# A fused attention and FP4-feed-forward layer: each block of P times V issued as two halves by queries, behind the third and the fourth softmax tile of a key block

## The chip, the cores and the metric

The kernel runs on one core of a Trainium2 chip. The metric is the device time of one execution in microseconds (us), as the median of the runs shown. A profiled execution gives the rows that are read below.

## The reference, cut to what matters

```python
# x (4, 2048, 256), 16 heads of 16, rotary tables for the last 1369 positions
qkv = (x @ w_qkv + b_qkv).reshape(b, n, 3, H, DH).transpose(2, 0, 3, 1, 4)
...
attn = softmax(einsum('bhqd,bhkd->bhqk', q, k) * scale)      # 64 heads, each 2048 x 2048
out = einsum('bhqk,bhkd->bhqd', attn, v)
x = layernorm(x + out @ w_proj + b_proj)
# feed-forward: inputs and weights rounded blockwise to FP4
x = layernorm(x + fp4_linear(silu(fp4_linear(x, w_gate)) * fp4_linear(x, w_up), w_down))
```

## The kernel before, in words

The kernel has three stages: the projections with the rotary step (up to about 330 us), attention over 64 heads (to about 3100 us), and the output projection with the feed-forward part. The change lies in the attention stage alone. There the code is written out straight, head after head, and each engine works through its own queue in the order in which it is written. Engines wait for each other by semaphores.

TensorE (PE in the profile) does three kinds of work in this stage:

- **S tiles** (`s_tile`, line 563): 128 queries against 512 keys, from partitions 64 and up of `qst` and `kst`. They serve only to find each query's maximum. Two S tiles fill two neighbouring banks of PSUM. VectorE (DVE) then reduces the pair to one maximum for each query (line 927, 128x1024 elements). There are four S banks, so two pairs. The first tile of a pair waits for `s_done`, that is for the reduction of the pair two before. Here the pair of the first two S tiles of a key block is called **the first pair**, the other **the second pair**.
- **T tiles** (`t_tile`, line 594): 128 keys against 512 queries, with the maxima as extra rows, from partitions 0 to 50 of the same tiles. ScalarE (ACT) takes the exponential of each into `pt` (line 772) and counts `p_ready`. The T tiles go through three banks in turn, so each T tile waits until ACT has read the third one before it (`t_bank_free`).
- **P times V** (`pv`, line 605): the 128x32 block of V (16 columns of V, one of ones for the sums, the rest zero) against 2048 queries, in four matmuls of 512 queries. Each goes to its own 32 partitions of bank 7, so the four use different columns of the array. They are float32, and each leaves two MATMUL records, so a call of `pv` shows as x8. The last matmul counts `pv_step`.

A **key block** is 128 keys, 16 in a head (`KT`). In `head`, each key block issues S, T four times over, the S tiles for a later head (20 tiles ahead), and then the `pv` of the key block before. S and T tiles use different rows of the array, and run side by side. Here S1 to S4 and T1 to T4 are the tiles of a key block in that order. S3 is the one that waits for the reduction of the second pair of the key block before.

Two places in each head differ from that pattern. In key block 1 (the second), `pv` starts a new head and so waits for `o_out`, the copy of the last head's result out of bank 7. ACT makes this copy (line 763) behind the first exponential of that key block. In key block 12, behind T4, TensorE transposes the maxima of the next head (`m_tile`, line 584, which also takes a T bank). In the last head no S tiles are left, and in the one before only 11 of 16 key blocks have them.

Of the kernel before, what the change touches and what calls it, by code (L numbers as in the profile page):

```python
# [31 lines left out]
G = B * H  # L32
# [6 lines left out]
CHUNK = 512  # L39
CHUNKS = N // CHUNK  # L40
NCH = B * CHUNKS
KT = N // P
# [20 lines left out]
TILES_S = KT * CHUNKS  # L63
PAIRS = TILES_S // 2
S_BANKS, T_BANKS, O_BANK = 4, 3, 7
# [2 lines left out]
AHEAD = 20  # L68

M_AFTER = 51  # L70
VAR_STEPS = 6
LN_STEPS = 6

# [35 lines left out]
def wait_after(eng, sem, value):  # L109

    if not isinstance(value, int) or value > 0:
        eng.wait_ge(sem, value)
# [37 lines left out]
def t_place(g, i):  # L150

    return 1 + g * (TILES_S + 1) + i + (i > M_AFTER)


def m_place(g):

    return 0 if g == 0 else 1 + (g - 1) * (TILES_S + 1) + M_AFTER + 1

# [16 lines left out]
def each_head(fn):  # L175

    for g in range(G):
        fn(At(0, g))


def layer_kernel(nc, x, xT, sinT, cosT, w_qk, w_v, b_qk, b_v, w_proj, b_proj, w_gate, w_up, w_down, eye, out):
    nc.disable_value_cache = True
    ctx = ExitStack()
    with ctx:
# [3 lines left out]
        def sem(name):  # L188
            return ctx.enter_context(nc.semaphore(name))
# [11 lines left out]
        ps = ctx.enter_context(nc.psum_tensor("ps", [P, 8, 512], F32))  # L201
# [66 lines left out]
        pt = [take(N) for _ in range(2)]  # L268
        vs = [take(KT * 32, "p (t d) -> p t d", t=KT) for _ in range(2)]
# [48 lines left out]
        mt_psum, mt_out, t_psum, p_ready = (sem(n) for n in ("mt_psum", "mt_out", "t_psum", "p_ready"))  # L318
        pv_step, v_staged, o_out, inverted = (sem(n) for n in ("pv_step", "v_staged", "o_out", "inverted"))
# [171 lines left out]
        def _(pe):  # L491
# [62 lines left out]
            def s_tile(g, i):  # L554

                pair = i // 2
                if i == 0:
                    pe.wait_ge(s_in[g.u % 2], g.quad(128, 64 * (g.u // 2 + 1)))
                if i % 2 == 0 and not (g.static(0) and pair < 2):
                    pe.wait_ge(s_done, g.times(PAIRS, pair - 1))  # L560
                qt, kc = i // CHUNKS, i % CHUNKS
                q, k = qst[g.u % 2], kst[g.u % 2]
                mm = nc.tensor.matmul(ps[:, i % S_BANKS, :], q[SROW:SROW + STACK, qt * P:(qt + 1) * P],  # L563
                                      k[SROW:SROW + STACK, kc * CHUNK:(kc + 1) * CHUNK], start=True, stop=True)
                if i % 2:
                    mm.then_inc(s_psum, 1)

            def t_bank_free(place):
# [5 lines left out]
                g, i = divmod(back - 1, TILES_S + 1)  # L574
                if back == 0 or i == M_AFTER + 1:
                    pe.wait_ge(mt_out, 1 if back == 0 else g + 2)
                else:
                    pe.wait_ge(p_ready, g * TILES_S + i - (i > M_AFTER) + 1)

            def m_tile(g):  # L580

                pe.wait_ge(m_split, g + 1)
                t_bank_free(m_place(g))
                nc.tensor.transpose(ps[0:MROWS * KT, t_bank(m_place(g)), 0:P // 2].bitcast(BF16),
                                    mp[g % 2].rearrange("p j q -> p (j q)"), ident16[:, :]).then_inc(mt_psum, 1)

            def t_tile(g, kb, qb):

                i = kb * CHUNKS + qb
                if i == 0:  # L590
                    pe.wait_ge(t_in[g.u % 2], g.quad(128, 64 * (g.u // 2 + 1)))
                    pe.wait_ge(m_in[g.c % 2], 16 * MROWS * (g.c // 2 + 1))
                t_bank_free(t_place(g.c, i))
                nc.tensor.matmul(ps[:, t_bank(t_place(g.c, i)), :], kst[g.u % 2][0:ROWS, kb * P:(kb + 1) * P],  # L594
                                 qst[g.u % 2][0:ROWS, qb * CHUNK:(qb + 1) * CHUNK],
                                 start=True, stop=True).then_inc(t_psum, 1)

            def pv(g, kb):

                if kb == 0:  # L600
                    pe.wait_ge(v_staged, g.times(1, 1))
                    wait_after(pe, o_out, g.times(1))
                pe.wait_ge(p_ready, g.times(TILES_S, CHUNKS * (kb + 1)))
                for qb in range(CHUNKS):
                    mm = nc.tensor.matmul(ps[32 * qb:32 * qb + 32, O_BANK, :], vs[g.u % 2][:, kb, :],  # L605
                                          pt[kb % 2][:, qb * CHUNK:(qb + 1) * CHUNK],
                                          start=(kb == 0), stop=(kb == KT - 1))
                mm.then_inc(pv_step, 1)

            def head(g):  # L610


                nxt, after = g.back(-1), g.back(-2)
                for kb in range(KT):
                    for qb in range(CHUNKS):
                        i = kb * CHUNKS + qb + AHEAD
                        if i < TILES_S and not g.static(G - 1):
                            s_tile(nxt, i)
                        elif i >= TILES_S and not g.static(G - 1) and not g.static(G - 2):
                            s_tile(after, i - TILES_S)  # L620
                        t_tile(g, kb, qb)
                        if kb * CHUNKS + qb == M_AFTER and not g.static(G - 1):
                            m_tile(g.c + 1)
                    if kb:
                        pv(g, kb - 1)
                    elif not g.static(0):
                        pv(g.back(1), KT - 1)

            for i in range(TILES_S):
                s_tile(At(0, 0), i)  # L630
# [5 lines left out]
            pe.wait_ge(v_out, 2 * NCH)  # L636
            pe.wait_ge(bias_done, 1)
            each_head(head)
            pv(At(0, G - 1), KT - 1)


            pe.wait_ge(o_out, G)
# [54 lines left out]
        def _(act):  # L697
# [54 lines left out]
            def maxima(g):  # L752

                act.wait_ge(mt_psum, g + 1)
                if g >= 2:
                    act.wait_ge(m_in[g % 2], 16 * MROWS * (g // 2))
                nc.scalar.activation(m_rows[g % 2], ps[0:MROWS * KT, t_bank(m_place(g)), 0:P // 2].bitcast(BF16), ACT.Copy
                                     ).then_inc(mt_out, 1)

            def out_of_psum(g):  # L760
                act.wait_ge(pv_step, g.times(KT, KT))
                act.wait_ge(o_store[g.u % 2], g.quad(32 * CHUNKS, 16 * CHUNKS * (g.u // 2 + 1)))
                nc.scalar.activation(ost[g.u % 2], ps[:, O_BANK, :], ACT.Copy).then_inc(o_out, 1)

            def head(g):
                for kb in range(KT):

                    wait_after(act, pv_step, g.times(KT, kb - 1))
                    for qb in range(CHUNKS):
# [4 lines left out]
                        if not g.static(0) and kb == 1 and qb == 0:  # L774
                            out_of_psum(g.back(1))
                        if i == M_AFTER and not g.static(G - 1):
                            maxima(g.c + 1)
# [45 lines left out]
            def deviation(n, alone):  # L823
                if group := norm_group(n, alone):
                    e, cols = group
                    act.wait_ge(var_step, e.quad(VAR_STEPS, VAR_STEPS))
                    nc.scalar.activation(std[:, cols], var[:, cols], ACT.Sqrt).then_inc(std_done, 1)
# [9 lines left out]
        def _(dve):  # L837
# [110 lines left out]
            def variance(n, alone):  # L948
# [5 lines left out]
                e, cols = group  # L954
                at = lambda k: e.quad(VAR_STEPS, k)
                g_bn, g_var, g_sums, g_d = bn[:, cols], var[:, cols], sums[:, cols], ln_d[:, cols]
# [230 lines left out]
```

## Time and profile before

| | us |
|---|---|
| median of 3 runs | 3880.2 (3878.26 to 3880.56) |
| the profiled execution, its own time | 3876.52 |
| its span in the trace | 3874.7 |
| busy: TensorE matmuls / VectorE / ScalarE | 3617.4 / 3350.5 / 2527.9 |
| attention stage, by T1 of the first head and the last T4 | 330.8 to 3097.9 |
| span of one head by its first S load (1500.58 to 1543.79) | 43.21 |

PEld is TensorE's load of weights, which can overlap with PE, its matmuls. A row of the timeline has the start, the duration, the engine, the line, what is written and read, and in brackets the engine's idle time ahead and what ended it. The ends of matmuls are modelled. A merged row (x8) spans from the first start to the last end.

### The profile page before, as it was taken

The numbers are of one execution on the slowest core, as the hardware profiler recorded it, in microseconds if no ns is written. First come the engines' busy times: TensorE is split into PE (matmuls) and PEld (weight loads), VectorE is DVE, ScalarE is ACT, GpSimd is POOL, SyncE is SP. The second block draws the span as 40 slices with busy tenths as digits, with TensorE's granted clock in tenths as the row PEclk, the third lists the DMA queues.
The fourth block names the chain that finished last, engine by engine and source line by source line (L and its number), as shares of the span: only waits on it lengthen the run. The fifth ranks groups of instructions, "written<-read, shape, count | busy, mean of one in ns | idle before, by whom it ended". The sixth has DMA issues, their size and how long they took to land.

```text
span 3874.7 us, 56176 instructions
## 1 busy us (share of the span) xinstructions
PE 3617.4 (93%) x19560; PEld 1556.6 (40%) x19560; DVE 3350.5 (86%) x3879; ACT 2527.9 (65%) x4870; POOL 712.0 (18%) x883
## 2 busy tenths in 40 slices
PE   7769999999999999999999999999999978888887
PEld 4433333333333333333333333333333346656665
DVE  7998888888888888888888888888888379999997
ACT  4334777777777777777777777777777723333333
POOL 6870000000000000000000000000000045555554
PEclk9887999999999999999999999999999989999999
DMA  5441111111111111111111111111111111111110
GB/s 153 161 167 53 44 39 38 44 45 40 37 43 45 41 37 42 46 42 37 40 47 42 38 39 48 42 38 38 46 44 39 29 50 45 43 47 45 47 37 20
DMA packets 121153, 195.55 MB, mean 50 GB/s; under 512 B 28640, under 2 KB 83040, under 8 KB 108640
## 3 DMA queue, kind: packets, MB, share of 16 engines
q1 hardware_dynamic: 111712, 184.16, 14.2%
q10 hardware_dynamic: 9216, 8.39, 0.6%
q8 instruction: 140, 2.29, 0.2%
q14 instruction: 85, 0.70, 0.1%
HBM read 139.55 MB, written 51.38 MB: 49 GB/s over the span
## 4 chain that ended last, share of the span: by engine, by line
PE 70%; issue 10%; POOL 8%; DVE 7%; ACT 3%; DMA 1%; POOLq 0%; SPq 0%; ACTq 0%; DVEq 0%
PE ps L563 28%; PE ps L605 26%; PE ps L594 14%; POOL v_all L1130 2%; ACT arena L772 2%; DVE arena L904 2%; DVE arena L909 1%; POOL arena L1130 1%; POOL arena L1132 1%; POOL arena L1124 1%; POOL arena L1125 1%; DVE arena L927 1%; PE ps L679 1%; DVE arena L897 1%; POOL arena L1065 1%
## 5 line engine op out<-in xcount | busy, mean ns | idle before, releaser
L927 DVE TENSOR_REDUCE arena<-ps 128x1 f32<-128x1024 f32 x2048 | 2412.7, 1220 | 332.8 <-PE ps L563 326.5
L772 ACT ACTIVATE arena<-ps 128x512 f32<-128x512 f32 x4096 | 2122.0, 604 | 622.5 <-PE ps L594 622.4
L594 PE MATMUL ps<-qst,kst 51*128 51x512 f32 x4096 | 1529.7, 453 | 31.1 <-ACT arena L772 7.7
L563 PE MATMUL ps<-kst,qst 48*128 48x512 f32 x4096 | 1284.4, 433 | 27.5 <-DMA qst<-qk_parts 23.2
L605 PE MATMUL ps<-arena 128*32 128x512 f32 x8192 | 1092.5, 605 | 2.4
L563 PEld LDWEIGHTS ps<-kst,qst 48*128 48x128 f32 x4096 | 622.8, 187 | 1090.0 <-DVE arena L927 942.9
L594 PEld LDWEIGHTS ps<-qst,kst 51*128 51x128 f32 x4096 | 677.3, 184 | 493.6 <-ACT arena L772 491.5
L1107 POOL TENSOR_TENSOR arena<-arena,ones 128x16 bf16<-128x16 f32 x64 | 14.2, 222 | 2640.5 <-DVE arena L932 2640.5
L605 PEld LDWEIGHTS ps<-arena 128*32 128x32 f32 x8192 | 163.0, 108 | 245.3 <-ACT arena L772 148.9
L689 PE MATMUL ps<-wdT,arena 128*128 128x256 f32 (+1 forms) x768 | 191.0, 400 | 36.1 <-ACT arena L810 36.1
L679 PE MATMUL ps<-wgT,arena 128*128 128x352 f32 x512 | 202.3, 478 | 3.5 <-DVE v_all L1037 2.5
L679 PE MATMUL ps<-wuT,arena 128*128 128x352 f32 x512 | 198.6, 470 | 0.0
L803 ACT ACTIVATE arena<-ps 128x256 f32<-128x256 f32 x64 | 24.5, 383 | 247.3 <-PE ps L657 247.3
L689 PEld LDWEIGHTS ps<-wdT,arena 128*128 128x128 f32 (+1 forms) x768 | 146.0, 197 | 69.9 <-ACT arena L810 42.0
L820 ACT ACTIVATE v_all<-ps 128x352 f32<-128x352 f32 x128 | 56.6, 462 | 122.8 <-PE ps L679 121.4
L1130 POOL TENSOR_TENSOR v_all<-v_all 128x352 f32<-128x352 f32 x128 | 119.3, 932 | 60.4 <-DVE v_all L868 60.4
L536 PE MATMUL ps<-arena 128*128 128x512 f32 x256 | 117.5, 613 | 12.6 <-DMA arena<-in_b_qk 9.4
L679 PEld LDWEIGHTS ps<-wuT,arena 128*128 128x128 f32 x512 | 100.5, 196 | 57.7 <-issue 6.2
L679 PEld LDWEIGHTS ps<-wgT,arena 128*128 128x128 f32 x512 | 97.7, 198 | 56.9 <-ACT arena L803 6.8
L735 ACT ACTIVATE arena<-ps,arena 128x512 f32<-128x512 f32 x64 | 41.2, 700 | 116.2 <-DMA qk_parts<-arena 105.2
L543 PE MATMUL ps<-arena 128*128 128x256 f32 x256 | 69.5, 432 | 40.5 <-ACT v_all L726 40.5
L1130 POOL TENSOR_TENSOR arena<-arena 128x256 f32<-128x256 f32 x64 | 59.7, 932 | 254.0 <-DVE arena L868 254.0
(101 smaller groups left out, 2282.7 us busy)
## 6 DMA issues: line engine op xcount, KB each, us to landing
qk_parts<-arena SPq DMA_DIRECT2D x32, 1024.0 KB, 7.4
kst<-qk_parts SPq DMA_DIRECT2D x128, 256.0 KB
qst<-qk_parts SPq DMA_DIRECT2D x128, 256.0 KB
kst<-qk_parts SPq DMA_DIRECT2D x128, 128.0 KB
qst<-qk_parts SPq DMA_DIRECT2D x128, 128.0 KB
att<-arena SPq DMA_DIRECT2D x256, 34.0 KB
arena<-in_xT SPq DMA_DIRECT2D x16, 512.0 KB, 8.2
arena<-att SPq DMA_DIRECT2D x128, 64.0 KB
```

What stands on the lines that cost most here:

```text
L536: mm = nc.tensor.matmul(ps[:, m, :], wqk[:, c, m * P:(m + 1) * P], xt[p][:, c], start=(c == 0), stop=(c == CT - 1))
L543: mm = nc.tensor.matmul(ps[:, 4 + v, t * C:(t + 1) * C], xt[p][:, c, (2 * v + t) * P:(2 * v + t + 1) * P], wv[:, c], start=(c == 0), stop= ...
L563: mm = nc.tensor.matmul(ps[:, i % S_BANKS, :], q[SROW:SROW + STACK, qt * P:(qt + 1) * P], k[SROW:SROW + STACK, kc * CHUNK:(kc + 1) * CHUNK ...
L594: nc.tensor.matmul(ps[:, t_bank(t_place(g.c, i)), :], kst[g.u % 2][0:ROWS, kb * P:(kb + 1) * P], qst[g.u % 2][0:ROWS, qb * CHUNK:(qb + 1) ...
L605: mm = nc.tensor.matmul(ps[32 * qb:32 * qb + 32, O_BANK, :], vs[g.u % 2][:, kb, :], pt[kb % 2][:, qb * CHUNK:(qb + 1) * CHUNK], start=(kb ...
L679: mm = nc.tensor.matmul(ps[:, bank, 0:FH], xhT_r[n.u % 2][:, ct], w[:, ct, hf * FH:(hf + 1) * FH], start=(ct == 0), stop=(ct == CT - 1))
L689: mm = nc.tensor.matmul(ps[:, 7, 0:C], hT_r[n.u % 2][0:nf, j], wdT[0:nf, k], start=(j == 0), stop=(j == 5))
L772: nc.scalar.activation(pt[kb % 2][:, qb * CHUNK:(qb + 1) * CHUNK], ps[:, t_bank(t_place(g.c, i)), :], ACT.Exp).then_inc(p_ready, 1)
L820: nc.scalar.activation(e_r[n.u % 2][:, hf * FH:(hf + 1) * FH], ps[:, 2 + 2 * hf, 0:FH], ACT.Silu).then_inc(e_done, 1)
L904: nc.vector.tensor_tensor(x, x, rot[p], ALU.add).then_inc(qr_done, 1)
L927: nc.vector.tensor_reduce(mx[g.u % 2][:, i // 2, i % 2:i % 2 + 1], ps[:, bank:bank + 2, :].rearrange("p b t -> p (b t)"), AX.X, ALU.max).t ...
L1130: nc.gpsimd.tensor_tensor(t, t, m, ALU.subtract).then_inc(step, 1)
```

## The change

`pv` takes a third argument `half`, and computes 256 of each 512 queries: four matmuls of 256 columns in place of four of 512, twice. `HALF_AFTER = (2, 3)` puts the first half behind T3 and the second behind T4. The waits for `v_staged`, `o_out` and `p_ready` stand ahead of the first half, and `pv_step` is counted by the second. The first half of the first key block is the only one that starts the bank anew. The lines behind move by a few: S is L565, T is L596 and `pv` is L609 in the changed kernel.

```diff
+HALF_AFTER = (2, 3)
...
-            def pv(g, kb):
-
-                if kb == 0:
+            def pv(g, kb, half):
+
+                if kb == 0 and half == 0:
                     pe.wait_ge(v_staged, g.times(1, 1))
                     wait_after(pe, o_out, g.times(1))
-                pe.wait_ge(p_ready, g.times(TILES_S, CHUNKS * (kb + 1)))
+                if half == 0:
+                    pe.wait_ge(p_ready, g.times(TILES_S, CHUNKS * (kb + 1)))
+                first = half * CHUNK // 2
                 for qb in range(CHUNKS):
-                    mm = nc.tensor.matmul(ps[32 * qb:32 * qb + 32, O_BANK, :], vs[g.u % 2][:, kb, :],
-                                          pt[kb % 2][:, qb * CHUNK:(qb + 1) * CHUNK],
-                                          start=(kb == 0), stop=(kb == KT - 1))
-                mm.then_inc(pv_step, 1)
+                    mm = nc.tensor.matmul(ps[32 * qb:32 * qb + 32, O_BANK, first:first + CHUNK // 2], vs[g.u % 2][:, kb, :],
+                                          pt[kb % 2][:, qb * CHUNK + first:qb * CHUNK + first + CHUNK // 2],
+                                          start=(kb == 0 and half == 0), stop=(kb == KT - 1 and half == 1))
+                if half:
+                    mm.then_inc(pv_step, 1)
...
-                    if kb:
-                        pv(g, kb - 1)
-                    elif not g.static(0):
-                        pv(g.back(1), KT - 1)
+                        if qb in HALF_AFTER:
+                            if kb:
+                                pv(g, kb - 1, HALF_AFTER.index(qb))
+                            elif not g.static(0):
+                                pv(g.back(1), KT - 1, HALF_AFTER.index(qb))
...
-            pv(At(0, G - 1), KT - 1)
+            for half in range(2):
+                pv(At(0, G - 1), KT - 1, half)
```

The queue of TensorE in an ordinary key block before, with the semaphores waited for (x3 and x4 merge equal rows; a matmul of `pv` stands here once, not twice):

```order
1012 L563 MATMUL ps<-kst,qst 128x512 [waits s_done]
1013 L594 MATMUL ps<-qst,kst 128x512 [waits p_ready]
1014 L563 MATMUL ps<-kst,qst 128x512
1015 L594 MATMUL ps<-qst,kst 128x512 [waits p_ready]
1016 L605 MATMUL ps<-arena 32x512 [waits p_ready]
1017 L605 MATMUL ps<-arena 32x512 x3
1018 L563 MATMUL ps<-kst,qst 128x512 [waits s_done]
```

S3, T3, S4 and T4 stand together, then the whole of `pv`, then the next S1. The same stretch, S3 to the next S1, in the changed kernel:

```order
1027 L565 MATMUL ps<-kst,qst 128x512 [waits s_done]
1028 L596 MATMUL ps<-qst,kst 128x512 [waits p_ready]
1029 L609 MATMUL ps<-arena 32x256 [waits p_ready]
1030 L609 MATMUL ps<-arena 32x256 x3
1031 L565 MATMUL ps<-kst,qst 128x512
1032 L596 MATMUL ps<-qst,kst 128x512 [waits p_ready]
1033 L609 MATMUL ps<-arena 32x256 x4
1034 L565 MATMUL ps<-kst,qst 128x512 [waits s_done]
```

A half now stands between S3 and S4, the two tiles of the second pair, and the other where the whole was. TensorE's queue at key block 1 of a head, from S3 on, before:

```order
952 L563 MATMUL ps<-kst,qst 128x512 [waits s_done]
953 L594 MATMUL ps<-qst,kst 128x512 [waits p_ready]
954 L563 MATMUL ps<-kst,qst 128x512
955 L594 MATMUL ps<-qst,kst 128x512 [waits p_ready]
956 L605 MATMUL ps<-arena 32x512 [waits p_ready,o_out,v_staged]
957 L605 MATMUL ps<-arena 32x512 x3
```

And the same in the changed kernel:

```order
1016 L565 MATMUL ps<-kst,qst 128x512 [waits s_done]
1017 L596 MATMUL ps<-qst,kst 128x512 [waits p_ready]
1018 L609 MATMUL ps<-arena 32x256 [waits p_ready,o_out,v_staged]
1019 L609 MATMUL ps<-arena 32x256 x3
1020 L565 MATMUL ps<-kst,qst 128x512
1021 L596 MATMUL ps<-qst,kst 128x512 [waits p_ready]
```

The wait for `o_out` has moved ahead of S4 and T4.

## Rows read from the trace of the kernel before

**Rows 1.** The page: busy us (share of the span) xinstructions of each engine.

```profile
PE 3617.4 (93%) x19560; PEld 1556.6 (40%) x19560; DVE 3350.5 (86%) x3879; ACT 2527.9 (65%) x4870; POOL 712.0 (18%) x883
```

**Rows 2.** Table by stretch: attention stage; one head (us, busy (instructions), clock, DMA share, GB/s).

```profile
340.00:3100.00 2760.00, 2721.30 (x16331) 967.66 (x16323) 2378.84 (x2126) 2147.45 (x4211) 76.78 (x315) 1.00 0.11 41
...
1500.58:1543.79 43.21, 42.74 (x262) 15.21 (x258) 38.04 (x35) 33.66 (x66) 1.22 (x5) 1.00 0.12 42
```

**Rows 3.** Timeline of one ordinary key block, all engines.

```profile
1510.40 1.06 PE L605 MATMUL ps<-arena 128*32 128x512 f32 x8
...
1511.40 0.50 PE L563 MATMUL ps<-kst,qst 48*128 48x512 f32 x1
...
1511.40 0.50 PE L594 MATMUL ps<-qst,kst 51*128 51x512 f32 x1
...
1511.74 0.39 PE L563 MATMUL ps<-kst,qst 48*128 48x512 f32 x1
...
1511.90 0.18 PEld L563 LDWEIGHTS ps<-kst,qst 48*128 48x128 f32 x1 [0.21 <-DVE arena L927]
...
1511.97 0.43 PE L563 MATMUL ps<-kst,qst 48*128 48x512 f32 x1
...
1512.00 2.06 ACT L772 ACTIVATE arena<-ps 128x512 f32<-128x512 f32 x4 [0.61 <-PE ps L594]
...
1512.17 2.36 DVE L927 TENSOR_REDUCE arena<-ps 128x1 f32<-128x1024 f32 x2 [0.32 <-PE ps L563]
1512.25 0.40 PE L563 MATMUL ps<-kst,qst 48*128 48x512 f32 x1
1512.65 0.18 PEld L594 LDWEIGHTS ps<-qst,kst 51*128 51x128 f32 x1 [0.46 <-ACT arena L772]
...
1513.08 0.16 PEld L605 LDWEIGHTS ps<-arena 128*32 128x32 f32 x8 [0.25 <-ACT arena L772]
...
1514.08 0.18 PEld L563 LDWEIGHTS ps<-kst,qst 48*128 48x128 f32 x1 [0.84 <-DVE arena L927]
```

**Rows 4.** Timeline of VectorE: the second pair's reduction of the key block before.

```profile
1510.63 1.22 DVE L927 TENSOR_REDUCE arena<-ps 128x1 f32<-128x1024 f32 x1
```

**Rows 5.** Two matmul groups at full clock, outside attention: 512 and 352 float32 columns.

```profile
199.53 5.74 PE L536 MATMUL ps<-arena 128*128 128x512 f32 x13
...
3603.06 0.76 PE L679 MATMUL ps<-wgT,arena 128*128 128x352 f32 x2
3603.65 0.75 PE L679 MATMUL ps<-wuT,arena 128*128 128x352 f32 x2
```

**Rows 6.** Timeline of key block 1 of a head: TensorE's loads and ScalarE.

```profile
1503.26 0.18 PEld L563 LDWEIGHTS ps<-kst,qst 48*128 48x128 f32 x1 [0.84 <-DVE arena L927]
...
1505.02 0.19 PEld L605 LDWEIGHTS ps<-arena 128*32 128x32 f32 x8 [0.32 <-issue]
1506.04 0.18 PEld L563 LDWEIGHTS ps<-kst,qst 48*128 48x128 f32 x1 [0.84 <-DVE arena L927]
...
1503.87 0.60 ACT L772 ACTIVATE arena<-ps 128x512 f32<-128x512 f32 x1 [0.62 <-PE ps L594]
1504.36 0.59 ACT L763 ACTIVATE arena<-ps 128x512 f32<-128x512 f32 x1
```

**Rows 7.** Timeline of TensorE's loads in key block 12 of a head.

```profile
1532.80 0.18 PEld L563 LDWEIGHTS ps<-kst,qst 48*128 48x128 f32 x1 [0.84 <-DVE arena L927]
...
1534.60 0.10 PEld L584 LDWEIGHTS ps<-ident,arena 128*48 128x48 bf16 x1 [0.37 <-issue]
...
1535.77 0.18 PEld L563 LDWEIGHTS ps<-kst,qst 48*128 48x128 f32 x1 [0.84 <-issue]
```

**Rows 8.** Timeline of TensorE's matmuls in the last head, without S tiles.

```profile
3093.97 0.96 PE L594 MATMUL ps<-qst,kst 51*128 51x512 f32 x3
3095.21 0.50 PE L594 MATMUL ps<-qst,kst 51*128 51x512 f32 x1 [0.28 <-ACT arena L772]
...
3096.64 0.96 PE L594 MATMUL ps<-qst,kst 51*128 51x512 f32 x3
```

## The prediction

> **What bounds the kernel now.** I read the page first: TensorE is busy for 93% of the span, VectorE for 86%, ScalarE for 65% [rows 1]. In the attention stage by itself the shares are 99%, 86% and 78%, with the clock at 1.00, its 2.4 GHz level [rows 2]. TensorE looks full there, but its busy time counts matmuls that overlap and fill in slowly, so the timeline must decide. One key block starts with the loads of S1 and T1 at 1511.40 and the next at 1514.08, which with the unrounded starts is a period of 2.675 us [rows 3]. One head takes 43.21 us [rows 2].
>
> Follow the chain in that block [rows 3]. T1 starts at 1511.40. Its exponential starts at 1512.00. T4 needs the bank that this exponential reads, and its load starts at 1512.65. P times V follows .43 later (1513.08), and the next S1 and T1 1.00 after that (1514.08). So .60 + .65 + .43 + 1.00 = 2.68: this is what sets the period. T4 had waited, since the load engine was idle for 0.46 and ACT ended it. ACT itself idles for 0.61 in each block, and VectorE for 0.32.
>
> A second loop runs beside it, with slack. The reduction of the second pair of the block before starts at 1510.63 and lasts 1.22, to 1511.85 [rows 4]. The load of S3 starts at 1511.90, .05 later, and VectorE is named as what ended 0.21 of idle time [rows 3]. So S3 does wait for VectorE, but its matmul starts at 1511.97, when the two pairs ahead have barely streamed. Once the halves are in, this is the loop that matters.
>
> **The change, part by part.**
>
> *The cost of a half.* A float32 matmul of 512 columns takes (5.74 - .59)/12 = .43 from start to start, where .59 is the length of the last one, 5.74 less twelve equal steps; two of 352 columns take 3603.65 - 3603.06 = .59, so .295 each [rows 5]. Both are .84 ns a column. A whole `pv` is two such rounds of four matmuls side by side: 2 x .43 = .86, and it lasts 1.00 to the next S1 [rows 3]. The other .14 is hand-over. A half has two rounds of 256 columns, .43, and the same hand-over: .57. No row shows a half. It can't cost under its streaming, .43, which also excludes a negative price, nor more than the whole, 1.00. If the hand-over halved too it would be .50. I take .57, the value built from the nearest row with only the column count changed, and .50 to .62 for the range.
>
> By the Trainium skill (TensorEngine Tiling, Key Properties) a change of tiling mode drains TensorE. By that rule each half pays the drain in full, which is .57, and without it the half would be .50. The .14 beyond streaming agrees with it.
>
> *What TensorE alone would take.* From S1's load to the end of three pairs side by side there are no gaps: S3's matmul starts .57 after S1 and lasts .43 (1511.97 against 1511.40), and a new kind of work starts .07 before the last matmul's end, as T4's .50 from 1512.65 against 1513.08 shows [rows 3]. So the first half starts at .93, or .90 where S3 needs not wait. The half ends at 1.47 (.90 + .57). S4 and T4, fresh behind a half, take .43 to the next hand-over, as T4 does now, and the second half .57: .90 + .57 + .43 + .57 = 2.47. T4 no longer waits, since its exponential has been read by 1.25. That would be .21 less per block than 2.675. The ACT chain, which sets the period now, is gone from the path, and ACT has 2.06 of work per block [rows 3].
>
> *What is late next: VectorE's loop.* The first half now stands between S3 and S4, which are one pair. The reduction of that pair can start only when both are done, and the next S3 can start only when that reduction is done. From rows:
> - start of the second pair's reduction to the load of the next S3: 1511.90 - 1510.63 = 1.27 [rows 3, 4];
> - load of S3 and T3 to the first half: .43, as from T4's load to `pv` [rows 3];
> - the first half: .57;
> - load of S4 to the start of the reduction: S1 lasts .50 from its load when it starts fresh, and a reduction starts .04 behind the end of its pair (S2 ends at 1511.74 + .39 = 1512.13, the reduction starts at 1512.17) [rows 3]: .54.
>
> The sum is 2.81, or 2.805 with the thirds of decimals kept. It is longer than 2.47 and than 2.675. Before, the same loop was no limit: S4 was done .75 behind S3's load (1512.25 + .40), while the first pair's reduction still ran to 1513.35, so VectorE's own 2.36 was all it held. With the halves VectorE idles ahead of the second pair: its first reduction starts .77 behind S1 and ends 1.18 later, S4 comes .4 after that. The new steady state has S3 loading .81 behind S1 (2.805 less .43 + .57 + .43 + .57 = 2.00), not .50.
>
> *Per head.* Sixteen blocks at +.13 are +2.08. Key block 1: the first half waits for the copy of the old head, which ends so that `pv` loads at 1505.02, 1.76 behind S1 at 1503.26 (ACT's exponential from 1503.87, then the copy from 1504.36 for .59) [rows 6]. The first half is due at .81 + .43 = 1.24, so it waits .52, and S4 and its reduction stand behind it in the queue: the loop is lengthened by all of it. Before, this block took 2.78 (1503.26 to 1506.04), .11 over the others: +.41 net. Key block 12 takes 2.97 now (1532.80 to 1535.77), .30 over [rows 7]. After the change the transposed maxima delay only T4's side and the next S1; S3 has .31 of slack there (.81 against .50), so the .30 is absorbed: -.30. VectorE's small reductions of a head fit into its new idle time at nothing. Sum: +2.19.
>
> Heads 0 to 61 give 62 x 2.19 = +136. Head 62 has S tiles in 11 blocks: 11 x .13 + .41, less 5 blocks x .21 at TensorE's pace = +.8. Head 63 has none: its 16 blocks go from 2.67 (3093.97 to 3096.64) [rows 8] to 2.47, -3.3, and the copy is waited for 1.76 - .90 = .86 instead of .11, +.75: -2.5. In all +134. Projections and feed-forward part are untouched; loads and semaphores of other queues only get more time. 3876.5 + 134 = 4010.5 for the profiled execution, which lies 3.7 below the median of the runs: 4014 for the median.
>
> With a half at .50 the block is 2.735, key block 1 +.46, a head 44.2, and in the last two heads more is won: +57, so 3937. At .62 it is 2.855 and +.57, a head 46.2: +190, so 4070.
>
> **The rivals.**
>
> *Weights loaded ahead.* S4's weights could be loaded during the half, and S4 would then take .39, as pipelined matmuls do, not .50 [rows 3]. The loop is then 2.70, a head about 43.8 with key block 1: 62 x .56 less 2 = +33, 3913. Against it: the next S1 could have loaded from 1510.7 on, when the first pair's reduction had given way to the second's (1510.63) [rows 4], and yet it loaded at 1511.40, at the end of `pv` [rows 3].
> The Trainium skill (TensorE: Matmul & The Clock Gate, Step-by-step) says that loads are pulled ahead of running matmuls when row groups don't conflict or the load goes to the background weight buffer; the trace disagrees at this hand-over.
>
> *Faster: TensorE sets the pace.* If the second loop doesn't close, because the second pair's banks come free earlier than I read, the block takes 2.47. A head is then 16 x 2.47 + .86 for the copy and .17 for the maxima = 40.6, 63 x -2.6 - 2.5 = about -168: 3712. The point is a loop under 2.675, that is a half under .44; between .43 and .44 the change wins a little, and well below that only with a shorter way from reduction to S3. For it speaks that TensorE looks full and T4's wait goes away. Against it: in every block shown S3's load starts .05 behind the end of that reduction.
>
> *The halves are not half.* If 256 columns cost as much as 512, a block is .90 + 1.00 + .43 + 1.00 = 3.33 by TensorE alone: about +650, 4530. The .84 ns a column at two sizes speaks against it.
>
> **How the numbers follow.** About 0.2% is what a measurement of this kernel can tell from no change. Chances: the VectorE loop as computed .81; weights ahead .06; TensorE's pace, faster, .07; a half near .44, so that all cancels, .03; halves not half .03. The range takes the first two and the bounds of the half: 3910 to 4072. Faster .07, same .03, slower .90.
>
> **What would show it.** In the changed trace: two rows of `pv` in each block, .57 from load to next load; blocks 2.80 apart, key block 1 at 3.32 and key block 12 with the next one at 5.6 for the two; S3's load ended by VectorE, .81 behind S1, with idle time of some .3 ahead of it; VectorE idle ahead of the second pair's reduction too; T4's wait for ACT gone. I am wrong if blocks stand at 2.47, if S4 loads before the half ends, or if the half is far from .57.

## The result

The changed kernel takes 4039.1 us as the median of four runs (4023.0 to 4050.0), against 3879.3 before: a ratio of 1.041, with a 95% interval of 1.037 to 1.045. It is slower by 4.1%. The forecast was 4014, 3.5% slower. The profiled execution took 4050.0 us with a span of 4048.2, 173.5 more than the span before.

The page after; the first line answers to [rows 1]. The second and third are the chain that ended last, by engine and by line, and the fourth is the group of the S reductions (count | busy, mean ns of one | idle time before them, who ended it):

```profile
PE 3721.7 (92%) x27752; PEld 1610.1 (40%) x27752; DVE 3435.6 (85%) x3879; ACT 2638.8 (65%) x4870; POOL 712.4 (18%) x883
...
PE 43%; DVE 36%; issue 11%; POOL 8%; DMA 1%; SPq 1%; ACT 0%; POOLq 0%; DVEq 0%; ACTq 0%
DVE arena L934 29%; PE ps L565 25%; PE ps L609 16%; POOL v_all L1137 2%; DVE arena L911 2%; DVE arena L916 1%; POOL arena L1137 1%; PE ps L596 1%; POOL arena L1139 1%; POOL arena L1131 1%; POOL arena L1132 1%; DVE arena L904 1%; PE ps L686 0%; DMA qst<-qk_parts 0%; POOL v_all L1139 0%
...
L934 DVE TENSOR_REDUCE arena<-ps 128x1 f32<-128x1024 f32 x2048 | 2501.4, 1222 | 405.0 <-PE ps L565 398.8
```

The same two lines of the chain before:

```profile
PE 70%; issue 10%; POOL 8%; DVE 7%; ACT 3%; DMA 1%; POOLq 0%; SPq 0%; ACTq 0%; DVEq 0%
PE ps L563 28%; PE ps L605 26%; PE ps L594 14%; POOL v_all L1130 2%; ACT arena L772 2%; DVE arena L904 2%; DVE arena L909 1%; POOL arena L1130 1%; POOL arena L1132 1%; POOL arena L1124 1%; POOL arena L1125 1%; DVE arena L927 1%; PE ps L679 1%; DVE arena L897 1%; POOL arena L1065 1%
```

VectorE is now on the chain for 36% of the span, against 7% before. Nearly all of it are the S reductions (29%, against 1%), though VectorE's busy share fell from 86% to 85%. That is the mark of a loop: an engine that sets the time and also idles (405 us ahead of these reductions). T tiles have all but left the chain (L594 had 14%, L596 has 1%). Their loads hardly wait for ScalarE any more (load groups of T tiles before, then after):

```profile
L594 PEld LDWEIGHTS ps<-qst,kst 51*128 51x128 f32 x4096 | 677.3, 184 | 493.6 <-ACT arena L772 491.5
...
L596 PEld LDWEIGHTS ps<-qst,kst 51*128 51x128 f32 x4096 | 684.5, 186 | 30.2 <-ACT arena L779 27.6
```

One ordinary key block after, TensorE's loads and VectorE, which answers to [rows 3] (start, duration, engine, line):

```profile
1540.01 0.18 PEld L565 LDWEIGHTS ps<-kst,qst 48*128 48x128 f32 x1 [0.41 <-issue]
...
1540.83 0.18 PEld L565 LDWEIGHTS ps<-kst,qst 48*128 48x128 f32 x1 [0.52 <-DVE arena L934]
...
1541.26 0.16 PEld L609 LDWEIGHTS ps<-arena 128*32 128x32 f32 x8 [0.25 <-ACT arena L779]
...
1541.83 0.18 PEld L565 LDWEIGHTS ps<-kst,qst 48*128 48x128 f32 x1 [0.41 <-issue]
...
1542.26 0.16 PEld L609 LDWEIGHTS ps<-arena 128*32 128x32 f32 x8 [0.24 <-issue]
...
1542.36 1.23 DVE L934 TENSOR_REDUCE arena<-ps 128x1 f32<-128x1024 f32 x1 [0.35 <-PE ps L565]
...
1542.83 0.18 PEld L565 LDWEIGHTS ps<-kst,qst 48*128 48x128 f32 x1 [0.41 <-issue]
...
1543.64 0.18 PEld L565 LDWEIGHTS ps<-kst,qst 48*128 48x128 f32 x1 [0.52 <-DVE arena L934]
```

Read the loop from these rows. S3 loads at 1540.83, .82 behind S1. VectorE is named as what ended its wait, and the load engine had been idle for .52 (the prediction said some .3). The first half starts .43 later (1541.26) and lasts .57 (to 1541.83). S4 loads there, and the reduction of its pair starts .53 later (1542.36). It lasts 1.23, to 1543.59, and the next S3 loads at 1543.64. The sum is .43 + .57 + .53 + 1.28 = 2.81, and that is the period.

Key block 1 after, which answers to [rows 6]: TensorE's loads, then ScalarE.

```profile
1525.41 0.18 PEld L565 LDWEIGHTS ps<-kst,qst 48*128 48x128 f32 x1 [0.41 <-issue]
...
1526.23 0.18 PEld L565 LDWEIGHTS ps<-kst,qst 48*128 48x128 f32 x1 [0.52 <-DVE arena L934]
...
1527.17 0.19 PEld L609 LDWEIGHTS ps<-arena 128*32 128x32 f32 x8 [0.75 <-issue]
1527.77 0.18 PEld L565 LDWEIGHTS ps<-kst,qst 48*128 48x128 f32 x1 [0.41 <-issue]
...
1528.77 0.18 PEld L565 LDWEIGHTS ps<-kst,qst 48*128 48x128 f32 x1 [0.41 <-issue]
```

```profile
1526.51 0.59 ACT L770 ACTIVATE arena<-ps 128x512 f32<-128x512 f32 x1
```

The first half was due .43 behind S3, at 1526.66, and loads at 1527.17, behind the copy: 1.76 behind S1. The block lasts 3.36.

The last head brought what the prediction did not have. Of the changed kernel, by stretch (us, busy (instructions) of PE, PEld, DVE, ACT, POOL, then the granted clock, DMA share, GB/s): the 63 heads ahead of the last, the start of the last head, and most of the rest of it.

```profile
340.00:3205.00 2865.00, 2760.08 (x24172) 999.26 (x24174) 2458.39 (x2126) 2222.97 (x4146) 76.78 (x315) 1.00 0.11 39
3207.00:3212.00 5.00, 4.19 (x35) 1.53 (x37) 0.00 (x0) 4.36 (x9) 0.00 (x0) 0.97 0.01 2
3215.00:3270.00 55.00, 55.00 (x256) 19.46 (x252) 0.25 (x1) 27.08 (x51) 0.00 (x0) 0.50 0.12 30
```

Of the kernel before, the last head:

```profile
3057.00:3097.00 40.00, 35.71 (x182) 12.22 (x181) 0.25 (x1) 31.47 (x61) 0.00 (x0) 1.00 0.17 44
```

Before, the clock stayed at 1.00 (2.4 GHz) there. After, it went to 0.50 (1.2 GHz) 5.3 us into the head, and key blocks took 4.32, not the 2.45 of the first. From its first S1 or T1 to the last T4 the last head took 41.3 us before and 65.0 after.

### The profile page after: what moved, and what is told of

Same layout as the page of the kernel before. It is cut to its first block, busy times and chain, and to the rows that moved or that the text cites. A ratio compares the mean times of both kernels' runs of the same rounds, so it can differ in the third digit from the quotient of the medians.

```text
span 4048.2 us, 72560 instructions
## 1 busy us (share of the span) xinstructions
PE 3721.7 (92%) x27752; PEld 1610.1 (40%) x27752; DVE 3435.6 (85%) x3879; ACT 2638.8 (65%) x4870; POOL 712.4 (18%) x883
## 4 chain that ended last, share of the span: by engine, by line
PE 43%; DVE 36%; issue 11%; POOL 8%; DMA 1%; SPq 1%; ACT 0%; POOLq 0%; DVEq 0%; ACTq 0%
DVE arena L934 29%; PE ps L565 25%; PE ps L609 16%; POOL v_all L1137 2%; DVE arena L911 2%; DVE arena L916 1%; POOL arena L1137 1%; PE ps L596 1%; POOL arena L1139 1%; POOL arena L1131 1%; POOL arena L1132 1%; DVE arena L904 1%; PE ps L686 0%; DMA qst<-qk_parts 0%; POOL v_all L1139 0%
## 5 line engine op out<-in xcount | busy, mean ns | idle before, releaser
L934 DVE TENSOR_REDUCE arena<-ps 128x1 f32<-128x1024 f32 x2048 | 2501.4, 1222 | 405.0 <-PE ps L565 398.8
L779 ACT ACTIVATE arena<-ps 128x512 f32<-128x512 f32 x4096 | 2231.0, 598 | 684.0 <-PE ps L596 681.6
L565 PE MATMUL ps<-kst,qst 48*128 48x512 f32 x4096 | 1776.4, 477 | 103.9 <-DMA qst<-qk_parts 23.8
L596 PE MATMUL ps<-qst,kst 51*128 51x512 f32 x4096 | 1772.4, 475 | 0.0
L609 PE MATMUL ps<-arena 128*32 128x256 f32 x16384 | 1325.9, 396 | 30.0 <-issue 30.0
L565 PEld LDWEIGHTS ps<-kst,qst 48*128 48x128 f32 x4096 | 685.7, 187 | 1391.5 <-issue 854.6
L596 PEld LDWEIGHTS ps<-qst,kst 51*128 51x128 f32 x4096 | 684.5, 186 | 30.2 <-ACT arena L779 27.6
L609 PEld LDWEIGHTS ps<-arena 128*32 128x32 f32 x16384 | 326.1, 108 | 533.5 <-issue 305.2
L538 PE MATMUL ps<-arena 128*128 128x512 f32 x256 | 116.1, 608 | 13.0 <-DMA arena<-in_b_qk 10.3
```

The costliest lines, as they stand in the source:

```text
L538: mm = nc.tensor.matmul(ps[:, m, :], wqk[:, c, m * P:(m + 1) * P], xt[p][:, c], start=(c == 0), stop=(c == CT - 1))
L609: mm = nc.tensor.matmul(ps[32 * qb:32 * qb + 32, O_BANK, first:first + CHUNK // 2], vs[g.u % 2][:, kb, :], pt[kb % 2][:, qb * CHUNK + firs ...
L779: nc.scalar.activation(pt[kb % 2][:, qb * CHUNK:(qb + 1) * CHUNK], ps[:, t_bank(t_place(g.c, i)), :], ACT.Exp).then_inc(p_ready, 1)
L934: nc.vector.tensor_reduce(mx[g.u % 2][:, i // 2, i % 2:i % 2 + 1], ps[:, bank:bank + 2, :].rearrange("p b t -> p (b t)"), AX.X, ALU.max).t ...
```

## The experiments

Times are medians of the runs; a number from one run is called so. "A block" is an ordinary key block, "a head" the distance from one head's first load to the next. The kernel before stands at 2.675 and 43.2, the changed one at 2.81 and 45.55.

### Halves between the pairs

```diff
-HALF_AFTER = (2, 3)
+HALF_AFTER = (1, 3)
```

> The changed kernel with the halves behind T2 and T4, so that no half stands between S3 and S4. Same matmuls, same count of hand-overs. Theory (the half between S3 and S4 closes a loop through VectorE): S3 and S4 stream side by side again, the loop is gone, and TensorE sets the pace: a key block of about 2.47 us (T1, T2: .66; half .57; T3, T4 .66; half .57), VectorE at 2.36 of 2.47. Key block 1 loses 1.09, since the first half now comes .66 behind S1 and the copy is free only 1.76 behind it. A head is about 40.8 against 43.2 before: some 150 us faster than the kernel before, near 3730. Rival (the halves cost by themselves, by their hand-overs and their doubled instructions, wherever they stand): a block stays above 2.675 and the kernel is slower than before.

Measured: 3742.4 us (3729.9 to 3758.1), a ratio of 0.964 (0.960 to 0.967). A block is 2.467, key block 1 3.59, a head 40.79. TensorE's loads and the other two engines from S1 on:

```profile
1502.80 0.18 PEld L565 LDWEIGHTS ps<-kst,qst 48*128 48x128 f32 x1 [0.41 <-DVE arena L934]
...
1503.40 2.26 ACT L779 ACTIVATE arena<-ps 128x512 f32<-128x512 f32 x4 [0.21 <-PE ps L596]
1503.46 0.16 PEld L609 LDWEIGHTS ps<-arena 128*32 128x32 f32 x8 [0.37 <-ACT arena L779]
...
1504.03 0.18 PEld L565 LDWEIGHTS ps<-kst,qst 48*128 48x128 f32 x1 [0.41 <-DVE arena L934]
...
1504.69 0.16 PEld L609 LDWEIGHTS ps<-arena 128*32 128x32 f32 x8 [0.37 <-issue]
...
1505.26 0.18 PEld L565 LDWEIGHTS ps<-kst,qst 48*128 48x128 f32 x1 [0.41 <-DVE arena L934]
```

.66 for a pair of S and T tiles, .57 for a half, and the same again: 2.46. The matmuls and hand-overs are those of the changed kernel, and it is 7% faster than that. So the loss comes from where the first half stands, not from the halves. The releaser named at each half's end is VectorE, but each load comes exactly .57 behind the half, so it is the half that sets it.

### Both halves where the whole stood

```diff
-HALF_AFTER = (2, 3)
+HALF_AFTER = (3, 3)
...
-                        if qb in HALF_AFTER:
+                        for half in range(2):
+                            if qb != HALF_AFTER[half]:
+                                continue
                             if kb:
-                                pv(g, kb - 1, HALF_AFTER.index(qb))
+                                pv(g, kb - 1, half)
                             elif not g.static(0):
-                                pv(g.back(1), KT - 1, HALF_AFTER.index(qb))
+                                pv(g.back(1), KT - 1, half)
```

> Both halves behind T4, one behind the other, where the whole stood before. Theory: the split by queries by itself costs nothing, a block is 2.68 and the kernel within some 5 us of the kernel before, apart from the last head. Rival (each half pays for itself, .14 of hand-over or more even where the kind of work doesn't change): a block of 2.82, some +145 us. A second question: does the granted clock fall to 0.50 in the last head, as it did in the changed kernel? If twice as many instructions cause that, yes; if the shorter period of that head does, no.

Measured: 3883.2 in one run, +4 on before. A block is 2.68, a head 43.25. TensorE's loads of both halves (x16) and of the next S1:

```profile
1502.23 0.59 PEld L609 LDWEIGHTS ps<-arena 128*32 128x32 f32 x16 [0.24 <-issue]
1503.23 0.18 PEld L565 LDWEIGHTS ps<-kst,qst 48*128 48x128 f32 x1 [0.41 <-issue]
```

Two halves in a row last 1.00 to the next S1, as the whole did, so the second pays no hand-over of its own. The .14 belongs to the change from one kind of work to the other. It is not all that one more change costs: a single pair of S and T tiles between two parts of `pv` takes .43, two take .66, and three take .89 (in the rows of the shortened reduction below). Each further pair costs .23, so a fresh start costs .20 more. The clock stayed up in the last head here.

### The reduction shortened, in both kernels

```diff
-                                            ps[:, bank:bank + 2, :].rearrange("p b t -> p (b t)"), AX.X, ALU.max
+                                            ps[:, bank + 1, :], AX.X, ALU.max
```

> The changed kernel, with VectorE reducing only the second bank of each pair (512 of 1024 elements), so the maxima are those of half the keys; everything else is as it was. The reduction should fall by some .5 us. Theory (the loop runs through the reduction): S3 is held no longer, the loop is 2.81 - .53 = 2.28, so TensorE's own 2.47 binds; a head falls from 45.55 to about 40.3 (16 x 2.47 + .86), and the kernel is faster than the kernel before by some 170 us. Rival (TensorE is longer with four hand-overs per block, VectorE only follows): the block stays at 2.81.

> The kernel before, with the same shortened reduction (512 of 1024 elements, the maxima are those of half the keys). Theory (before, T1, its exponential, T4 and the whole of P times V set the period, and VectorE had slack): a block stays at 2.67 to 2.68 and the kernel within 15 us of the kernel before. Rival (VectorE's share of the path was real before too): a block clearly under 2.67.

Measured: the changed kernel falls to 3692.0 in one run, below the kernel before, with blocks of 2.46 and heads of 40.43. The kernel before goes to 3865.9, and its blocks stay at 2.67 (heads 43.16). The changed kernel's rows:

```profile
1501.36 0.69 DVE L934 TENSOR_REDUCE arena<-ps 128x1 f32<-128x512 f32 x1 [1.44 <-PE ps L565]
...
1501.83 0.18 PEld L565 LDWEIGHTS ps<-kst,qst 48*128 48x128 f32 x1 [0.41 <-issue]
...
1502.17 0.18 PEld L565 LDWEIGHTS ps<-kst,qst 48*128 48x128 f32 x1
...
1502.72 0.16 PEld L609 LDWEIGHTS ps<-arena 128*32 128x32 f32 x8 [0.36 <-issue]
```

The reduction takes .69, S3 loads .34 behind S1 (1502.17) and is held by nothing, and the half starts .89 behind S1. Two S1 loads in a row of the kernel before, with the shortened reduction:

```profile
1501.33 0.18 PEld L563 LDWEIGHTS ps<-kst,qst 48*128 48x128 f32 x1 [0.84 <-DVE arena L927]
...
1504.00 0.18 PEld L563 LDWEIGHTS ps<-kst,qst 48*128 48x128 f32 x1 [0.84 <-DVE arena L927]
```

Half a reduction is worth .35 a block in the changed kernel and nothing in the kernel before (2.67 here too). That is the direct proof that VectorE came onto the path with the change. The block of 2.46 also shows that TensorE sets the pace in halves_1_3 (2.467), where a reduction still takes 1.22. The profiled execution of the kernel before got 10.6 us shorter, and 10.3 of them lie ahead of the first head (which starts at 320.5, not 330.8), where S tiles run alone and a shorter reduction does shorten the time.

### Unequal parts

```diff
-                first = half * CHUNK // 2
+                first, cols = ((0, 128), (128, 384))[half]
```

The second kernel has `((0, 384), (384, 128))` there. In both, `cols` takes the place of `CHUNK // 2` in the slices of the matmul.

> The changed kernel with unequal parts: the first 128 queries of each 512 behind T3, the other 384 behind T4. Theory (the part behind T3 lies on VectorE's loop with its full length): 128 columns less, two rounds, shorten the loop by 2 x .107 = .21, from 2.81 to 2.60; a head of about 42.7 against 45.55 with equal halves and 43.2 before: about 30 us faster than the kernel before, 3850, if the last head keeps its clock. Rival (what is lost is the number of hand-overs or the position): a head of 45.5 still.

> The changed kernel with the parts the other way round: 384 of each 512 queries behind T3, 128 behind T4. Theory (the part behind T3 lies on VectorE's loop with its full length): 128 columns more in each of two rounds, so the loop grows by .21 to 3.03 a block, a head of about 48.7 (45.55 with equal halves, 42.5 measured with 128 and 384), near 4220. Rival (what counts is that the cut falls there, and S4's reduction hides the rest): a head below 46.

Measured in one run each: 3830.8 with blocks of 2.60 and heads of 42.5; 4225.4 with blocks of 3.03 and heads of 48.8. Loads with 128 columns behind T3:

```profile
1501.04 0.18 PEld L565 LDWEIGHTS ps<-kst,qst 48*128 48x128 f32 x1 [0.30 <-DVE arena L934]
...
1501.47 0.16 PEld L609 LDWEIGHTS ps<-arena 128*32 128x32 f32 x8 [0.24 <-issue]
...
1501.82 0.18 PEld L565 LDWEIGHTS ps<-kst,qst 48*128 48x128 f32 x1 [0.20 <-issue]
...
1503.64 0.18 PEld L565 LDWEIGHTS ps<-kst,qst 48*128 48x128 f32 x1 [0.30 <-DVE arena L934]
```

The part takes .35 (1501.47 to 1501.82), .22 less than a half, and the block .21 less. With 384 columns behind T3 the part takes .78 and the block is .22 longer:

```profile
1500.41 0.16 PEld L609 LDWEIGHTS ps<-arena 128*32 128x32 f32 x8 [0.24 <-ACT arena L779]
1501.19 0.18 PEld L565 LDWEIGHTS ps<-kst,qst 48*128 48x128 f32 x1 [0.62 <-issue]
...
1503.01 0.18 PEld L565 LDWEIGHTS ps<-kst,qst 48*128 48x128 f32 x1 [0.73 <-DVE arena L934]
```

The S3 load ahead of this part stands at 1499.98, so the block is 3.03. At three sizes the block follows the part behind T3 one for one: 2.60, 2.81, 3.03. The first kernel came out 19 us under the 3850 expected, about 11 of them in its heads (42.5, not 42.7).

### The copy ahead of the exponential

```diff
+                        if not g.static(0) and kb == 1 and qb == 0:
+                            out_of_psum(g.back(1))
                         act.wait_ge(t_psum, g.times(TILES_S, i + 1))
                         nc.scalar.activation(pt[kb % 2][:, qb * CHUNK:(qb + 1) * CHUNK],
                                              ps[:, t_bank(t_place(g.c, i)), :], ACT.Exp).then_inc(p_ready, 1)
-                        if not g.static(0) and kb == 1 and qb == 0:
-                            out_of_psum(g.back(1))
```

> The halves behind T2 and T4, and ScalarE copies the old head's result ahead of the first exponential of key block 1 instead of behind it. Theory (key block 1 loses 1.12, since the first half waits for the copy): the copy now starts as soon as the last half of the old head is done, .17 behind S1, and is free .84 behind it; the half is due at .66. Key block 1 falls from 3.59 to about 2.8, with T4 held a little by the delayed exponential. 63 x .78 = about 49 less than halves_1_3, near 3693. Rival (that wait is hidden by VectorE's own 2.36 per block or comes back elsewhere in the head): a head stays near 40.8.

Measured: 3676.2 us (3674.8 to 3677.0), a ratio of 0.947 (0.946 to 0.949). Key block 1 is 2.79, a head 39.99, so .80 less a head and 50 us over 63 of them. The wait for the copy was real, and most of it comes off: key block 1 was 1.12 over the others and is still .32 over them. Its first half still waits for the copy, which ends at 1496.36, and loads .95 behind S1, not the .66 of other blocks (TensorE's loads, then ScalarE's copy):

```profile
1495.47 0.18 PEld L565 LDWEIGHTS ps<-kst,qst 48*128 48x128 f32 x1 [0.41 <-DVE arena L934]
...
1496.42 0.19 PEld L609 LDWEIGHTS ps<-arena 128*32 128x32 f32 x8 [0.66 <-issue]
...
1498.25 0.18 PEld L565 LDWEIGHTS ps<-kst,qst 48*128 48x128 f32 x1 [0.41 <-issue]
```

```profile
1495.75 0.61 ACT L770 ACTIVATE arena<-ps 128x512 f32<-128x512 f32 x1
```

The median fell by 66; the other 16 lie most likely in the clock of the last head, which fell in the profiled run of halves_1_3 and not in that of this kernel.

### The clock in the last head

Five kernels ask what brings the clock down there. The first two issue `pv` whole behind T4 in the last head, one with the changed order before it, one with halves_1_3 and the early copy:

```diff
-                        if qb in HALF_AFTER:
+                        if g.static(G - 1):
+                            if qb == CHUNKS - 1:
+                                pv(*((g, kb - 1) if kb else (g.back(1), KT - 1)), None)
+                        elif qb in HALF_AFTER:
```

> The changed kernel, but in the last head (which has no S tiles) P times V is issued whole behind T4, as before. In the trace of the changed kernel the clock went to its lower level 6 us into that head and the head took 65 us, not 39; the runs of the changed kernel spread over 27 us, those of before over 5. Theory (the halves in the head without S tiles bring the clock down in some executions): the last head takes about 42.8 at full clock, the profile falls to about 4024, the spread to a few us, and the median to about 4022. Rival (the low clock is the work of the 63 heads ahead, or of chance): it falls in the last head here too, and the spread stays.

> As copy_first_1_3, with P times V whole in the last head. Theory: at full clock the last head takes about 42.8 instead of 39.5, or of the 60 and more that it takes where the clock falls; so it is about 3685 with a spread of a few us, against a spread of 20 to 30 us for copy_first_1_3 and a median some 10 to 25 higher there. Rival: the clock falls in the last head here too; both have the same spread.

Measured: 4027.6 (4024.5 to 4040.1), with the clock up in the last head of the profiled run (41.3 to its last T4, as before), and 3696.8 (3676.9 to 3703.1), with the clock down in its profiled run. The clock went down with P times V whole, so the halves don't decide it, and the theory fell. The last expectation also gave copy_first_1_3 a spread of 20 to 30 us, and its four runs spread over 2.

The other three add S matmuls that nobody reads, in the last head and the last three key blocks of the one before:

```diff
+                        elif g.static(G - 1) or kb >= 13:
+                            filler(g, kb, qb)
...
+            def filler(g, kb, qb):
+
+                if g.static(G - 2) and kb == 13 and qb == 0:
+                    pe.wait_ge(s_done, G * PAIRS)
+                nc.tensor.matmul(ps[:, qb, :], qst[g.u % 2][SROW:SROW + STACK, kb * P:(kb + 1) * P],
+                                 kst[g.u % 2][SROW:SROW + STACK, qb * CHUNK:(qb + 1) * CHUNK], start=True, stop=True)
```

> The changed kernel, plus S matmuls that nobody reads in the last head and the last three key blocks of the one before (they use the upper rows of the array beside the T tiles, and no engine waits for them). Theory (without S tiles TensorE does less per microsecond in the last head, and the clock may then fall, by chance from run to run; how P times V is cut doesn't decide it): no run loses its clock there, the last head takes about 39 in the profile, all runs lie within some 6 us near 4021, where the changed kernel spread from 4023 to 4050. Rival (the clock falls for another reason at the end of the stage): the spread of 25 us stays.

> copy_first_1_3_last_whole, whose last head fell to the lower clock in the profile and whose runs spread from 3677 to 3703, with the same unread S matmuls at the end. Theory (S tiles beside the T tiles keep the clock): all runs within some 6 us, near 3678. Rival: the spread of 26 us stays.

> copy_first_1_3 with the same unread S matmuls at the end, as the best version that the runs point to. Theory: as copy_first_1_3, 3675, with a spread of a few us also over more runs; the S matmuls run beside the T tiles and cost nothing. Rival: they lengthen the last head by what the pairs take more than T tiles alone, below 3 us.

Measured over five runs each: 4023.7 (4022.5 to 4032.5), 3678.3 (3677.7 to 3682.4) and 3676.0 (3674.8 to 3677.9). The last head of the kernel with the whole `pv`, without the filler and with it:

```profile
2862.00:2917.00 55.00, 54.72 (x166) 17.45 (x167) 0.25 (x1) 27.89 (x55) 0.00 (x0) 0.52 0.13 32
```

```profile
2862.00:2899.00 37.00, 36.25 (x224) 13.94 (x223) 0.25 (x1) 28.51 (x56) 0.00 (x0) 1.00 0.19 48
```

With the filler the spread of this pair went from 26 us to 5, and the clock was at 1.00 in all three profiled last heads. The S matmuls cost nothing visible: 3676.0 against 3676.2. The 4032.5 of after_filler is its profiled run. There the lower clock at the start of the stage lasted until 381 us, and the first head took 60.7. So the clock varies at that end too: over all fourteen profiles it rose between 328 and 381 us. The runs with the filler speak for the fuller array as what holds the clock in the last head, but it isn't shown. The kernel before and copy_first_1_3 kept it without the filler, by their profiles and by the narrow spread of their total times, and in an execution without a profile only the total time tells.

## Why the prediction was right, and where it was off

- **The mechanism.** The half between S3 and S4 closes a loop through VectorE. Six kernels bear it out: the moved half, the adjoining halves, the shortened reduction in both orders, and two other sizes. The forecast terms .43, .57, .54 and 1.27 measured .43, .57, .53 and 1.28.
- **The half at .57** was right, and with it the choice against .50. So was the reason: two halves in a row cost 1.00, so .14 is paid for each change of the kind of work. By the Trainium skill (TensorEngine Tiling (Array Packing), Key Properties) that is the drain at a change of tiling mode, and the trace agrees: 1.00 for two halves in a row, .57 for a half by itself.
- **Key block 1** was forecast at 3.32 and took 3.36; the half came 1.76 behind S1, as computed. **Key block 12** with the next took 2.98 + 2.65 = 5.63, which is 2 x 2.81: the .30 of the transposed maxima is absorbed, as said.
- **The head** took 45.55 and not 45.40. The reduction, which now starts on an idle VectorE, lasts 1.23, not the 1.22 taken from one that follows another. .01 a block, 16 blocks, 62 heads: 9 us. (In the sum below it is 8, since the 61 heads before averaged 43.23 and not 43.21.)
- **The missing term** is the clock. I took it as 1.00 throughout the stage because it was so before, and named no rival for it. The range had room for its 26 us only because it was made wide for the price of a half, so that the median lies well inside owes something to luck. The sum over the profiled span shows what it cost. Start of the first head +1.4 and first head +6.1 (forecast +2.2): the lower clock lasted until 355 us, not 341. Heads 1 to 61: +141.7 (forecast +133.6). Head 62: +.7 (forecast +.8). Last head: +23.6 (forecast -2.5; the kernels with unequal parts, where the clock stayed up, took 39.0 and 39.4 there against 41.3, so that term was about right). The rest of the kernel: 776.8 both times, as forecast. In all +173.5. Without the last head's 26 the profiled execution would be at 4024, where the fastest run of the changed kernel (4023.0) and the runs with the filler (4023.7) are.
- **The rivals.** S4's weights weren't loaded ahead: the load at 1541.83 stands at the end of the half, as in the kernel before at the end of the whole. Within a run of S tiles a load does come early: S3's at 1511.90 lies under S2's matmul of 1511.74 to 1512.13 [rows 3]. So it is only at the hand-over that none does. TensorE's pace of 2.47 was right as a number (2.467 and 2.46 where the loop is gone), only not for this order. The halves not being half is excluded by the three sizes.

The likely idea of the change, to break the chain T1, exponential, T4, whole `pv` that set the period, works: T4's wait was gone. It needed the first half one tile earlier, and the copy moved. That version, copy_first_1_3, takes 3676, 5.3% less than before.

## What to carry to other kernels

Before moving work into a queue, ask which tiles on either side are consumed together: work put between the two tiles of one consumer's input lengthens that consumer's loop by its full length, and sets the time once that loop is the longest, even if the engine that it runs on could go faster. A loop can set the time with every engine on it idle part of it; add up its steps from one release to the next instead of comparing busy shares. A wait that costs nothing now (S3's .21) shows the loop that is next in line.

## What the runs showed that I had not expected

The clock of a dense stage can go down at its end, in some executions and not in others: the changed kernel's four runs spread over 27 us and halves_1_3's over 28, where those of the kernel before spread over 8 in all 27 of its runs. At the end of the stage I saw it only in the head without S tiles, in three profiles and each time 5 to 7 us into that head. In the changed kernel TensorE was busy for 84% of the time by the records (4.19 of 5.00 us) when the clock fell from 1.00 to 0.50, and it did not get the clock back in the 55 us that followed at 100% busy. The busy share alone doesn't tell the cases apart: in copy_first_1_3_last_whole it was 91% in the 3 us around the fall (2.72 of 3.00), and in the kernel before 88% over the first 10 us of that head (8.83 of 10.00), with no fall.

A single profiled execution says 24 us for the last head. How much of that a run pays varies from run to run. But it isn't chance alone: of the two kernels compared here only the changed one pays it. Why is open.
